# A Perceiver block on one Trainium2 core: ScalarE rounds the turned weights ahead of the next exponentials in the first half of each batch

## The chip, the cores and the metric

The kernel runs on one core of a Trainium2 chip. The metric is the device time of one execution in microseconds (us), the median over several runs.

## The reference

`x` is 64 sequences of 32 rows of 512 numbers, `ctx` is 64 sequences of 257 rows of 128. Three blocks follow each other, each on the layer-normed stream with a residual sum around it:

```python
x = x + xattn(layernorm(x), ctx, ...)   # 16 heads, latent queries and keys with rotary factors
x = x + attn(layernorm(x), ...)         # 16 heads of 32, weights from amp * cos(phase)
x = x + ffn(layernorm(x), ...)          # gates, two layers of folded products, layer norms
```

The change is in the middle of the first block. There, for a batch element b:

```python
scores  = einsum('hsr,hlr->hsl', q_r, k_r)     # 16 heads x 32 rows = 512 rows of 257 scores
weights = softmax(scores, axis=-1)
ctx_c   = einsum('hsl,ld->hsd', weights, kv_r)
```

and the result goes through an output product over all heads (`w_vo`).

## The kernel before

All operands of products are split into a high part (rounded to the float32r type) and a low part (value minus high), and a product is three matmuls (`multiply_parts`: high x high, high x low, low x high). ScalarE makes the high parts by a copy, VectorE or GpSimd the low parts by a subtraction (`low_part` on VectorE, line 77).

`query_path` carries the queries into DRAM. `cross_attention` then works through 64 batch elements, four to a tile of 128 output rows (`BT` = 4, `TILES` = 16). The 512 score rows of a batch element are taken in two halves of 256, each in two PSUM banks. So a tile has eight steps j = 0 to 7; step j belongs to batch `u = j // 2` and `half = j % 2`, and n counts steps over the whole stage. Below, a "first half" is an even step and a "second half" an odd one.

Each engine runs its own list of instructions in order, written out by hand, and waits on semaphores that count. In step n:

- **TensorE**: `score` of step n+1 (6 matmuls of 258 columns), `turn_weights` of step n (4 transposes of the normalised weights into the single bank `c_et_ps`; waits for `normed` of n and for `et_split` of n-1), in second halves `turn_kv` of the next batch, then `project` (matmuls of the output product of an earlier tile: one head in first halves, three heads in second halves), and in first halves `mix` of the batch before (6 matmuls).
- **ScalarE**: `exponential` of step n+1 (two activations with sums), `round_turned` of step n (reads `c_et_ps`), in second halves `round_kv`, `round_mixed` and `round_keys`, in first halves `round_queries`; at j = 4 also `square_row`.
- **VectorE**: `find_peak` of n+1, `keep_ends` of n, in first halves `split_kv`, in second halves `add_end` of the batch before, `normalise` of n+1 (a reciprocal and a product), `split_turned` of step n (the second reader of `c_et_ps`), at j = 2 `add_out` and at j = 6 `keep_moments`.
- **GpSimd**: rotates keys, takes the low parts of queries, keys and the mixed result.
- **SyncE**: all DMAs. The weight of key 257 goes through DRAM: after `keep_ends` of a second half, `store_ends` writes it, and `spread_ends` reads it back to all partitions; `add_end` of the next second half waits for it.

The last reader of `c_et_ps` gives the bank back:

```python
            def turn_weights(n, half):
                pe.wait_ge(normed, n + 1)
                wait(pe, et_split, n)
```

`c_sc_ps` has two banks for each half, and `c_et_ps` has one bank for both halves.

Of the kernel before, what the change touches and what calls it, by code (L numbers as in the profile page):

```python
# [42 lines left out]
def wait(engine, sem, value):  # L43

    if isinstance(value, int) and value <= 0:
        return
    engine.wait_ge(sem, value)
# [27 lines left out]
def low_part(nc, low, value, high):  # L75

    return nc.vector.tensor_tensor(low, value, high.bitcast(F32), ALU.subtract)  # L77
# [669 lines left out]
def cross_attention(nc, crossing, holo, x, q_dram, w_vo_dram, ends_dram, x1, spare, stat, ident, eps, half_pi, left_counted):  # L747
# [4 lines left out]
    with ExitStack() as ctx:  # L752
# [69 lines left out]
        def known(i, least):  # L822

            return not isinstance(i, int) or i >= least
# [94 lines left out]
        def _(dve):  # L919
            def find_peak(n, v):  # L920
                dve.wait_ge(scored, n + 1)
                wait(dve, exped, n - 1)
                nc.vector.tensor_reduce(peak[:, v], sc_ps[:, 2 * v:2 * v + 2, 0:L], AX_X, ALU.max, negate=True).then_inc(peaked, 1)  # L923
# [10 lines left out]
            def keep_ends(n, i, u, half):  # L934
                v = u % 2
                if half == 0:
                    wait(dve, ends_stored[v], 32 * i + 16 * (u // 2))
                nc.vector.tensor_tensor(ends[:, v, 2 * half:2 * half + 2], sc_ps[:, 2 * half:2 * half + 2, END], inverse[:, half],
                                        ALU.mult).then_inc(ended, 1)

            def split_turned(n, u, half):
                dve.wait_ge(et_rounded, n + 1)
                at = slice(2 * P * half, 2 * P * (half + 1))
                low_part(nc, e_t[1][:, u % 2, :, at], et_ps[:].rearrange("p (k x) -> p k x", k=2), e_t[0][:, u % 2, :, at]).then_inc(et_split, 1)

            def split_kv(b, u):
                dve.wait_ge(kv_rounded, b + 1)
                low_part(nc, kv[1][:, u], kv_ps[:, 0:2 * P].rearrange("p (k x) -> p k x", k=2), kv[0][:, u]).then_inc(kv_split, 1)

            def add_end(i, u):  # L950
                b, v = BT * i + u, u % 2
                dve.wait_ge(mix_done, b + 1)
                dve.wait_ge(ends_back[v], 32 * i + 16 * (u // 2) + 16)
                wait(dve, mix_split, b - 1)
                spread = ends_spread[:, v].rearrange("p (x c) -> p c x", c=CH)
                by_chunk = lambda a: a.rearrange("p (c x) -> p c x", c=CH)
                nc.vector.scalar_tensor_tensor(by_chunk(whole[:, v]), spread, kv_t[u][:, END:L], by_chunk(mix_ps[:]),
                                               ALU.mult, ALU.add).then_inc(mix_taken, 1)
# [15 lines left out]
            def tile(i, w):  # L974
                for j in range(STEPS):
                    n, u, half = STEPS * i + j, j // 2, j % 2
                    b = BT * i + u
                    more = not (isinstance(n, int) and n == PAIRS - 1)
                    if more:
                        find_peak(n + 1, 1 - half)  # L980
                    keep_ends(n, i, u, half)
                    if half == 0:
                        split_kv(b, u)
                    if half == 1 and (u or known(i, 1)):
                        add_end(i - (u == 0), (u - 1) % BT)
                    if more:
                        normalise(n + 1, 1 - half)
                    split_turned(n, u, half)
                    if j == 2 and known(i, 2):
                        add_out(i - 2)  # L990
                    if j == 6 and known(i, 2):
                        keep_moments(i - 2)
# [32 lines left out]
        @block.scalar  # L1025
        def _(act):
            def exponential(n, v):

                act.wait_ge(peaked, n + 1)
                for c in range(2):  # L1030
                    last = nc.scalar.activation(sc_ps[:, 2 * v + c, 0:L], sc_ps[:, 2 * v + c, 0:L], ACT.Exp, bias=peak[:, v, c:c + 1],  # L1031
                                                accum_out=total[:, v, c:c + 1])
                last.then_inc(exped, 1)

            def round_turned(n, b, u, half):
                act.wait_ge(turned, n + 1)
                if half == 0:
                    wait(act, mix_done, b - 1)
                nc.scalar.activation(e_t[0][:, u % 2, :, 2 * P * half:2 * P * (half + 1)], et_ps[:].rearrange("p (k x) -> p k x", k=2),
                                     ACT.Copy).then_inc(et_rounded, 1)  # L1040

            def round_kv(b, u):
                act.wait_ge(kv_turned, b + 1)
                wait(act, mix_done, b - BT + 1)
                nc.scalar.activation(kv[0][:, u], kv_ps[:, 0:2 * P].rearrange("p (k x) -> p k x", k=2), ACT.Copy).then_inc(kv_rounded, 1)

            def round_queries(b, u, t):
                act.wait_ge(q_loaded[u], queries_in(u, t))
                wait(act, scored, 2 * b - 2)
                nc.scalar.activation(q_high[:, u % 2], q[u].bitcast(F32), ACT.Copy).then_inc(q_rounded, 1)  # L1050

            def round_keys(b, u):
                act.wait_ge(rotated_, b + 1)
                wait(act, scored, 2 * b - 2)
                nc.scalar.activation(keys[0][:, u % 2], kv_even[u], ACT.Copy).then_inc(key_rounded, 1)

            def round_mixed(b, u, t, w):
                act.wait_ge(mix_taken, b + 1)
                if u == 0:
                    wait(act, out_done, t - 1)  # L1060
                nc.scalar.activation(mixed[0][:, w, :, u], whole[:, u % 2].rearrange("p (h s) -> p h s", h=H), ACT.Copy).then_inc(mix_rounded, 1)  # L1061

            def square_row(t):
                act.wait_ge(centred, t + 1)
                row = x1[:, bass.ds(t, 1)].rearrange("p t d -> p (t d)")
                if isinstance(t, int) and t == 0:
                    act.wait_ge(warmed, 1)
                nc.scalar.activation(scratch[:], row, ACT.Square, bias=neg_mean[:], accum_out=squares[:]).then_inc(squared, 1)

            def tile(i, w):  # L1070
                for j in range(STEPS):
                    n, u, half = STEPS * i + j, j // 2, j % 2
                    b = BT * i + u
                    if not (isinstance(n, int) and n == PAIRS - 1):
                        exponential(n + 1, 1 - half)
                    round_turned(n, b, u, half)
                    if half == 1 and not (isinstance(b, int) and b + 1 >= B):
                        round_kv(b + 1, (u + 1) % BT)
                    if half == 1 and (u or known(i, 1)):
                        round_mixed(b - 1, (u - 1) % BT, i if u else i - 1, w if u else 1 - w)  # L1080
                    if not (isinstance(b, int) and b + 2 >= B):
                        if half == 0:
                            round_queries(b + 2, (u + 2) % BT, i + (u + 2) // BT)
                        else:
                            round_keys(b + 2, (u + 2) % BT)
                    if j == 4 and known(i, 2):
                        square_row(i - 2)

            nc.scalar.activation(scratch[:, 0:1], ident[:, 0:1], ACT.Exp).then_inc(warmed, 1)
            round_keys(0, 0)  # L1090
            round_queries(0, 0, 0)
            exponential(0, 0)
            round_kv(0, 0)
            round_keys(1, 1)
            round_queries(1, 1, 0)
            in_tiles(act, tile)
            round_mixed(B - 1, BT - 1, TILES - 1, 1)
            act.wait_ge(holo_stepped, 12)
            nc.scalar.activation(holo.phase, holo.phase, ACT.Abs).then_inc(holo_cosined, 1)
            act.wait_ge(holo_cosined, 1)  # L1100
            nc.scalar.activation(holo.phase, holo.phase, ACT.Sin, bias=half_pi[:], scale=-1.0).then_inc(holo_cosined, 1)
            act.wait_ge(kept, TILES - 2)
            nc.scalar.activation(stat[:, 1, 0:TILES - 2], stat[:, 1, 0:TILES - 2], ACT.Sqrt, bias=eps[:], scale=1.0 / D).then_inc(rooted, 1)
            for t in (TILES - 2, TILES - 1):
                square_row(t)
# [1105 lines left out]
```

## Time and profile before

| | us |
|---|---|
| median of 3 runs | 1606.23 (1604.67 to 1607.58) |
| the profiled execution | 1605.91 |
| its span, first to last instruction | 1604.1 |
| full tiles of the attention loop, from j = 4 of tile 1 to j = 4 of tile 14 | 373.71 |
| the same, to the last transposes before the stop in tile 15 | 398.36 |
| one tile in the middle of it (801.00 to 829.70) | 28.70 |

In the span TensorE is busy 92%, VectorE 71%, ScalarE 54%, GpSimd 39%. Times inside the trace count from the start of the span. "T1" below stands for the four transposes of a first half, "T2" for those of a second half. A row of the timeline gives the start, the duration, the engine, the line, the operation with its output and inputs, how many instructions were merged, and in brackets the idle time of the engine in front of it with what ended it. Ends of matmuls are modelled.

### The profile page before, as it was taken

The page shows a single profiled execution, that of the slowest core. Times are in us where ns is not written, and L with a number is a line of the kernel's source. Part 1 is how long each engine was busy: PE and PEld are TensorE (multiplying, and loading weights), DVE is VectorE, ACT ScalarE, POOL GpSimd, SP SyncE. Part 2 cuts the span into 40 slices and gives each one's busy share as a digit, 9 for nine tenths or more (in the row PEclk, how much of TensorE's full clock was granted, in tenths as well). Part 3 has the DMA queues.
Part 4 walks back from the last instruction along what each step waited for, and adds up shares of the span by engine and source line. Part 5 has one row for each costly group of instructions (what it writes and reads, how often), then busy time and mean ns, then how long its engine had stood idle before and what let it go on. Part 6 is the DMA issues. An engine that isn't in the chain of part 4 may idle for free. (4 is left out here: it accounts for less than half of the span.)

```text
span 1604.1 us, 27410 instructions
## 1 busy us (share of the span) xinstructions
PE 1471.8 (92%) x8392; PEld 1134.6 (71%) x8392; DVE 1139.9 (71%) x1952; ACT 863.3 (54%) x1859; POOL 632.8 (39%) x596
## 2 busy tenths in 40 slices
PE   4799999999967999999999867999898899999997
PEld 3577777777746888888888656888443478787876
DVE  6888788887628888888888653777687735556466
ACT  4566566656546666666666533555211355554554
POOL 4244342542036777767677513221251202222021
PEclk9899999999979999999999978999898899999999
DMA  4223334243565555555555514000244100000000
GB/s 152 70 83 107 105 110 128 71 122 88 191 197 109 129 114 118 127 111 128 111 120 120 121 20 172 1 0 0 84 173 159 43 1 1 27 0 27 0 27 27
DMA packets 141207, 140.14 MB, mean 87 GB/s; under 512 B 84438, under 2 KB 112214, under 8 KB 139996
## 3 DMA queue, kind: packets, MB, share of 16 engines
q1 hardware_dynamic: 140572, 138.60, 31.9%
q10 hardware_dynamic: 576, 0.81, 0.2%
q8 instruction: 30, 0.49, 0.1%
q14 instruction: 29, 0.24, 0.1%
HBM read 109.88 MB, written 27.39 MB: 86 GB/s over the span
## 5 line engine op out<-in xcount | busy, mean ns | idle before, releaser
L1031 ACT ACTIVATE c_sc_ps<-c_sc_ps,c_peak 128x257 f32<-128x257 f32 x256 | 113.6, 444 | 156.9 <-DVE c_peak L923 156.9
L77 DVE TENSOR_TENSOR b_rot_parts_low<-b_rot,b_rot_parts_high 128x1536 fp32r<-128x1536 f32 x64 | 136.5, 2132 | 20.6 <-ACT b_rot_parts_high L543 20.6
L884 POOL TENSOR_TENSOR c_mixed_low<-c_whole,c_mixed_high 128x512 fp32r<-128x512 f32 x64 | 81.9, 1280 | 131.2 <-ACT c_mixed_high L1061 131.2
L280 POOL TENSOR_TENSOR b_turned_raw<-b_turn_part 128x384 f32<-128x384 f32 x32 | 69.0, 2155 | 163.5 <-DVE b_key_parts_low L77 162.2
L1627 PE MATMUL f_ps<-f_right,f_left 128*128 128x512 f32 x256 | 116.1, 615 | 8.3 <-ACT f_raw L1670 5.9
L70 PE MATMUL c_out_ps<-c_shared_high,c_mixed_high 128*128 128x512 f32 x256 | 112.6, 440 | 8.8 <-issue 8.8
L326 DVE TENSOR_TENSOR b_rot<-b_w_qr,b_angle 128x1536 f32<-128x1536 f32 x64 | 119.5, 1867 | 0.2
L923 DVE TENSOR_REDUCE c_peak<-c_sc_ps 128x2 f32<-128x514 f32 x128 | 88.5, 691 | 42.7 <-PE c_sc_ps L72 41.6
L70 PE MATMUL b_ps<-c_shared_high,b_wq_parts_high 128*128 128x512 f32 x256 | 108.6, 424 | 6.5 <-DVE c_shared_low L77 6.5
L276 POOL TENSOR_TENSOR b_turn_part<-b_early,b_centre 128x384 f32<-128x384 f32 x64 | 84.6, 1342 | 72.9 <-DMA b_early<-early 71.3
L70 PE MATMUL e_mm_ps<-folded_high,e_h_t_high 128*128 128x512 f32 x256 | 106.4, 416 | 6.7 <-DVE e_h_t_low L77 6.6
L1125 PE MATMUL c_et_ps<-ident,c_e 128*128 128x128 f32 x512 | 81.3, 282 | 32.9 <-DVE c_e_t_low L77 30.9
L543 ACT ACTIVATE b_rot_parts_high<-b_rot 128x1536 fp32r<-128x1536 f32 x64 | 95.3, 1489 | 24.5 <-PE b_ps L72 17.0
L1983 ACT ACTIVATE spare<-spare 128x512 f32<-128x512 f32 x64 | 46.3, 724 | 114.3 <-DVE spare L2050 114.3
L72 PE MATMUL b_ps<-c_shared_high,b_wq_parts_low 128*128 128x512 f32 x256 | 103.9, 406 | 0.0
L71 PE MATMUL b_ps<-c_shared_low,b_wq_parts_high 128*128 128x512 f32 x256 | 103.3, 404 | 0.0
L1627 PEld LDWEIGHTS f_ps<-f_right,f_left 128*128 128x128 f32 x256 | 50.0, 197 | 74.3 <-issue 65.1
L72 PE MATMUL c_out_ps<-c_shared_high,c_mixed_low 128*128 128x512 f32 x256 | 102.4, 400 | 0.0
L71 PE MATMUL e_mm_ps<-folded_low,e_h_t_high 128*128 128x512 f32 x256 | 102.3, 400 | 0.0
L72 PE MATMUL e_mm_ps<-folded_high,e_h_t_low 128*128 128x512 f32 x256 | 102.3, 399 | 0.0
L71 PE MATMUL c_out_ps<-c_shared_low,c_mixed_high 128*128 128x512 f32 x256 | 102.1, 399 | 0.0
L1863 POOL TENSOR_TENSOR spare<-spare,out_norm 128x512 f32<-128x512 f32 x15 | 20.8, 1389 | 200.5 <-DVE spare L2057 200.5
(244 smaller groups left out, 4291.1 us busy)
## 6 DMA issues: line engine op xcount, KB each, us to landing
c_ends_spread<-end_weights SPq DMA_DIRECT2D x64, 256.0 KB, 3.8
carried_queries<-x SPq DMA_DIRECT2D x7, 2048.0 KB, 11.2
b_early<-early SPq DMA_DIRECT2D x15, 640.0 KB, 4.0
c_raw<-cache_t SPq DMA_DIRECT2D x64, 128.5 KB, 3.4
c_swapped<-cache_t SPq DMA_DIRECT2D x128, 64.2 KB, 3.2
f_left<-ent_in SPq DMA_DIRECT2D x16, 512.0 KB, 5.5
f_right<-ent_out SPq DMA_DIRECT2D x16, 512.0 KB, 6.9
c_q_first<-carried_queries SPq DMA_DIRECT2D x32, 224.0 KB, 3.3
```

What stands on the lines that cost most here:

```text
L70: nc.tensor.matmul(out, left[0], right[0], start=start, stop=False)
L71: nc.tensor.matmul(out, left[0], right[1], start=False, stop=False)
L72: return nc.tensor.matmul(out, left[1], right[0], start=False, stop=stop)
L77: return nc.vector.tensor_tensor(low, value, high.bitcast(F32), ALU.subtract)
L276: nc.gpsimd.tensor_tensor(turn_part[:, n], key, centre[:, 2 * v + n].unsqueeze(2).to_broadcast(shape), ALU.mult).then_inc(key_multiplied, 1)
L326: nc.vector.tensor_tensor(rot[:, k % 2], weight, angles, ALU.mult).then_inc(rot_ready, 1)
L543: nc.scalar.activation(rot_parts[0][:, k % 2], rot[:, k % 2], ACT.Copy).then_inc(rot_rounded, 1)
L884: nc.gpsimd.tensor_tensor(mixed[1][:, w, :, u], whole[:, u % 2].rearrange("p (h s) -> p h s", h=H), mixed[0][:, w, :, u].bitcast(F32), ALU ...
L923: nc.vector.tensor_reduce(peak[:, v], sc_ps[:, 2 * v:2 * v + 2, 0:L], AX_X, ALU.max, negate=True).then_inc(peaked, 1)
L1031: last = nc.scalar.activation(sc_ps[:, 2 * v + c, 0:L], sc_ps[:, 2 * v + c, 0:L], ACT.Exp, bias=peak[:, v, c:c + 1], accum_out=total[:, v, ...
L1125: last = nc.tensor.transpose(et_ps[:, (2 * k + c) * P:(2 * k + c + 1) * P], e[:, half, c, k * P:(k + 1) * P], ident[:])
L1627: return nc.tensor.matmul(ps[:, m], left[:, slot, m * P:(m + 1) * P], right[:, slot], start=k == 0, stop=k == CF - 1)
```

## The change

In first halves ScalarE does `round_turned(n)` ahead of `exponential(n + 1)`, and VectorE does `split_turned(n)` right behind `keep_ends`, ahead of `split_kv` and `normalise(n + 1)`. Second halves keep their order. No instruction, semaphore, buffer or DMA is added or taken away.

```diff
@@ VectorE, tile(i, w), step j
                     keep_ends(n, i, u, half)
                     if half == 0:
+                        split_turned(n, u, half)
                         split_kv(b, u)
                     if half == 1 and (u or known(i, 1)):
                         add_end(i - (u == 0), (u - 1) % BT)
                     if more:
                         normalise(n + 1, 1 - half)
-                    split_turned(n, u, half)
+                    if half == 1:
+                        split_turned(n, u, half)
                     if j == 2 and known(i, 2):
                         add_out(i - 2)
@@ ScalarE, tile(i, w), step j
+                    if half == 0:
+                        round_turned(n, b, u, half)
                     if not (isinstance(n, int) and n == PAIRS - 1):
                         exponential(n + 1, 1 - half)
-                    round_turned(n, b, u, half)
+                    if half == 1:
+                        round_turned(n, b, u, half)
                     if half == 1 and not (isinstance(b, int) and b + 1 >= B):
                         round_kv(b + 1, (u + 1) % BT)
```

## Rows read from the trace of the kernel before

**Rows 1.** Windows, busy time by engine: 13 tiles, a batch of tile 0, four batches

```profile
core 0: us, PE busy (x) PEld busy (x) DVE busy (x) ACT busy (x) POOL busy (x), PEclk, DMA share, GB/s
513.40:887.11 373.71, 362.40 (x2081) 308.08 (x2081) 310.70 (x688) 249.92 (x752) 269.08 (x313) 1.00 0.56 120
485.60:491.96 6.36, 4.37 (x29) 3.71 (x29) 5.60 (x13) 4.63 (x14) 5.12 (x7) 1.00 0.66 134
801.00:807.92 6.92, 6.92 (x41) 5.93 (x41) 5.54 (x12) 5.34 (x16) 5.11 (x7) 1.00 0.51 106
807.92:814.89 6.97, 6.92 (x41) 5.94 (x41) 5.90 (x14) 4.64 (x14) 5.42 (x7) 1.00 0.64 121
814.89:822.00 7.11, 6.92 (x42) 5.92 (x41) 5.78 (x12) 4.64 (x14) 5.24 (x7) 1.00 0.71 149
822.00:829.70 7.70, 7.09 (x43) 5.91 (x41) 6.70 (x16) 4.63 (x14) 4.97 (x7) 1.00 0.42 96
```

**Rows 2.** Timeline of TensorE from 801 us, transposes alone: T1, T2, T1, T2

```profile
801.00 0.63 PE L1125 MATMUL c_et_ps<-ident,c_e 128*128 128x128 f32 x4 [0.42 <-DVE c_e_t_low L77]
...
804.30 0.60 PE L1125 MATMUL c_et_ps<-ident,c_e 128*128 128x128 f32 x4
...
807.92 0.63 PE L1125 MATMUL c_et_ps<-ident,c_e 128*128 128x128 f32 x4
...
811.40 0.63 PE L1125 MATMUL c_et_ps<-ident,c_e 128*128 128x128 f32 x4
```

**Rows 3.** Timeline of VectorE: a second half, a first half, and around add_out

```profile
804.50 0.69 DVE L923 TENSOR_REDUCE c_peak<-c_sc_ps 128x2 f32<-128x514 f32 x1 [0.47 <-PE c_sc_ps L72]
...
805.18 1.13 DVE L957 SCALAR_TENSOR_TENSOR c_whole<-c_ends_spread,c_kv_t,c_mix_ps 128x512 f32<-128x512 f32 x1
...
808.65 0.41 DVE L77 TENSOR_TENSOR c_kv_low<-c_kv_ps,c_kv_high 128x256 fp32r<-128x256 f32 x1
809.76 0.17 DVE L928 RECIPROCAL c_inverse<-c_total 128x2 f32<-128x2 f32 x1 [0.69 <-ACT c_sc_ps L1031]
809.96 0.69 DVE L931 TENSOR_TENSOR c_e<-c_sc_ps,c_inverse 128x512 f32<-128x512 f32 x1
810.57 0.68 DVE L77 TENSOR_TENSOR c_e_t_low<-c_et_ps,c_e_t_high 128x512 fp32r<-128x512 f32 x1
...
825.39 0.68 DVE L965 SCALAR_TENSOR_TENSOR x<-c_out_ps,x 128x512 f32 x1
...
826.28 0.69 DVE L923 TENSOR_REDUCE c_peak<-c_sc_ps 128x2 f32<-128x514 f32 x1
```

**Rows 4.** Timeline of ScalarE: an exponential of a second half, then a first half

```profile
805.23 0.45 ACT L1031 ACTIVATE c_sc_ps<-c_sc_ps,c_peak 128x257 f32<-128x257 f32 x1 [1.01 <-DVE c_peak L923]
...
808.70 0.45 ACT L1031 ACTIVATE c_sc_ps<-c_sc_ps,c_peak 128x257 f32<-128x257 f32 x1 [0.86 <-DVE c_peak L923]
...
809.62 0.60 ACT L1039 ACTIVATE c_e_t_high<-c_et_ps 128x512 fp32r<-128x512 f32 x1
810.10 0.64 ACT L1050 ACTIVATE c_q_high<-c_q_first 128x512 fp32r<-128x512 f32 x1
```

**Rows 5.** Timeline, last transposes of the stage: TensorE, then rounding, then low part

```profile
937.40 0.63 PE L1125 MATMUL c_et_ps<-ident,c_e 128*128 128x128 f32 x4 [0.72 <-DVE c_e_t_low L77]
...
938.06 0.60 ACT L1039 ACTIVATE c_e_t_high<-c_et_ps 128x512 fp32r<-128x512 f32 x1 [1.84 <-PE c_et_ps L1125]
...
938.69 0.69 DVE L77 TENSOR_TENSOR c_e_t_low<-c_et_ps,c_e_t_high 128x512 fp32r<-128x512 f32 x1 [0.20 <-ACT c_e_t_high L1039]
```

**Rows 6.** SyncE's queue from 805 us: the end weights out and back

```profile
805.44 0.36 SPq L831 DMA_DIRECT2D end_weights<-c_ends  x1
...
807.85 0.45 SPq L837 DMA_DIRECT2D c_ends_spread<-end_weights  x1
```

**Rows 7.** Tile c_ends_spread, 515 to 911 us: idle time before its reader (us, times)

```profile
  issue: 2.5, 5
  DMA c_ends_spread<-end_weights: 0.9, 3
...
DMA to landing us min/median/max: 3.3/3.8/5.1
```

## The prediction

> **What bounds the kernel now.** I read the busy times by window first. From 513.40 to 887.11, in 13 tiles, TensorE is busy 362.40 of 373.71 us at the full granted clock, so it is near its limit, and 3% is left [rows 1]. A clean tile is 28.70 us: four batches of 6.92, 6.97, 7.11 and 7.70. TensorE's busy time is 6.92 in the first three and 7.09 in the last, while the work is the same; the extra length lies in waits. In tile 0, where there is no output product yet, TensorE is busy 4.37 of 6.36 us: there a chain through the other engines sets the pace.
>
> Next I read where TensorE waits: at the transposes, for the low part of the transposes before [rows 2]. The order of one step on VectorE tells why. A step begins with `find_peak` and ends with `split_turned`, and the next transposes start 3.42 us after the peak began, in second halves (804.50 to 807.92) [rows 2, 3]. In first halves it is the same 3.42 from 807.98, where the peak began 0.06 after T1, to T2 at 811.40. But the contents differ. A second half has no gap: `add_end` of 1.13 us fills the time of the exponentials. A first half has a gap of 0.69 us, in which VectorE waits for the exponentials (809.76), and the low part of T1, ready to be made long before, comes last (810.57 to 811.25) [rows 3]. T2 starts 0.15 after it.
>
> TensorE alone needs less: after a T1 that had to wait itself, T2 comes 3.30 later with no wait (801.00 to 804.30) [rows 2]. After T2 its work lasts 3.49 (811.40 to the batch end at 814.89 [rows 1]). So TensorE's floor is 6.79 a batch.
>
> **The change part by part.** Let T1 start at 0.
>
> *New first half.* The rounding can start when the transposes are done. The last step of the stage is the one where ScalarE stands ready for them: rounding at 0.66, low part at 0.66 + 0.63 = 1.29 [rows 5]. `keep_ends` is over by then (its peak begins at 0.06 to 0.20 and both take about 0.8). On ScalarE the exponentials start 0.48 after the rounding (809.62 to 810.10), at 1.14; that is later than now, where they start when the peak is found, at 0.78 (808.70 less 807.92) [rows 2, 4]. From the first exponential to the reciprocal it takes 1.06 (808.70 to 809.76), so ScalarE lets VectorE go on at 2.20 [rows 3, 4]. On VectorE the low part takes 0.61 until the next one begins (as 809.96 to 810.57 shows for a product of that size), `split_kv` begins at 1.90 and ends at 2.31. The next one may begin 0.07 ahead of that end, at 2.24. So the reciprocal begins at 2.24, bounds 2.20 and 2.31. Product 0.20 later, at 2.44; it ends at 3.13, and T2 can start 0.15 behind it, at 3.28 (3.24 to 3.35).
>
> TensorE arrives at 3.30. So the wait for the low part goes, its successor is the wait for `normed`, and it ends within 0.1 of TensorE's own arrival. The exponentials of the second half are 0.36 later than before, and nothing pays for it up to there.
>
> *What is late next.* `score` of the next step stands ahead of T2 in TensorE's order, and ends 0.16 after T2's natural start; the next peak begins 0.20 after that start (804.30 to 804.50), at 3.50 [rows 2, 3]. VectorE is free for it at 2.44 + 0.61 = 3.05. The second half keeps its order and its 3.42. So T1 to T1 is 3.50 + 3.42 = 6.92, above TensorE's 6.79. That is what the first batch of the tile already does (6.92) [rows 1]; the change brings the next two to it, which gains 0.05 and 0.19.
>
> *The batch with `add_out`.* It holds VectorE for 0.89 (825.39 to 826.28) and the peak behind it is what makes this batch 7.70 [rows 1, 3]. It would now start at 3.05 instead of 3.39 (825.39 less 822.00). Peak at 3.94, next T1 at 7.36: a gain of 0.34. The two small copies of `keep_moments` have the 0.45 from 3.05 to 3.50 to themselves.
>
> *Sum.* A clean tile becomes 3 x 6.92 + 7.36 = 28.12, a gain of 0.58. From 513.40 to 911.76, where the last tile stops for its DMAs, are 398.4 us, 13.9 tiles of 373.71 / 13 = 28.75: 8.1 us. The bounds of T2 move only the last batch of a tile, by up to 0.07: 1.0 us.
>
> *Taken off.* In tile 0, T1 to T1 is now 6.36. New, VectorE is free for the peak at 3.05, and 3.42 later is 6.47: 0.11 lost in each of about 6 batches, 0.6 us. Then the end weights. `add_end` waits for them in 8 of 55 batches already, 3.4 us in all [rows 7]. In a clean batch they are stored at 805.44, read back at 807.85 and, with the median landing of 3.8, there at 811.65; `add_end` comes at 812.06, some 0.4 later [rows 6, 7]. Batches of 7.0 to 7.1 shrink to 6.92, and landings go up to 5.1. Where the DMA rules, a batch gives back what it gained. I take 12 of 55 (bounds 8 and 25), that is 1.8 us (1.2 to 3.7).
>
> Moving the rounding costs ScalarE and its other work nothing: `round_queries` starts 0.3 later (2.20 against 1.90), and ScalarE waits some 1 us for the next peak anyway (1.01 ahead of 805.23) [rows 4]. SyncE and GpSimd are moved past nothing.
>
> 8.1 - 0.6 - 1.8 = 5.7 us. The profiled execution took 1605.91, its span 1604.1; it lies 0.3 below the median of the runs. Forecast **1600.2**.
>
> **A rule weighed.** VectorE instructions start about 0.07 before the recorded end of the one before (809.96 + 0.69 is 810.65, the next starts at 810.57) [rows 3]. The Trainium skill, VectorE: DVE Perf Modes, section "The DRAIN you can't avoid", says that the next operation does not start until the pipe is empty. By that the two hand-overs of the new order would add 0.14, T2 could start at 3.42, and the gain would be 5.7 less 14 x 0.14, 3.7 us: an estimate by the page, which the trace's overlap speaks against.
>
> **The rivals.** *The end weights take it all.* If the average batch waits 0.15 more for its DMA, 55 x 0.15 = 8.2 us is lost, and the time is 1605.9 + 0.6, about **1606**. For it: the slack is 0.4 and the landings spread by 1.8; waits exist [rows 7]. Against it: the first batch of each clean tile has run at 6.92 and does not wait. With a loss of 5 us or more the change can't be told from none.
>
> *T2 is late: slower.* The exponentials now stand behind T1, the rounding and its latency, one chain from T1 to T2: 3.28 by my sum. TensorE needs 3.49 after T2, so the chain costs nothing until 6.92 - 3.49 = 3.43. Past that each 0.1 costs all 55 batches 5.5 us, and the gain is gone at about 3.43 + 0.58 / 4 = 3.58. It takes one hand-over or one slowed exponential 0.3 above its row. At 3.80 a batch is 7.29, the one with `add_out` 7.88, the tile 29.75, and the time 1606 + 13.9 x 1.05, about **1620**. Against it: each link has its row, the one that never waits in the middle of the stage, transposes to rounding, included [rows 5]. The new order lets VectorE read `c_et_ps` while ScalarE works in `c_sc_ps`; today `add_end` reads `c_mix_ps` beside the exponential of 805.23, which takes the same 0.45 as the one of 808.70 beside the shorter `split_kv` [rows 3, 4]. For it: it is the longest chain that the change makes, from five links that were never seen in this order.
>
> **How the numbers follow.** Forecast 0.60, end weights 0.25, late T2 0.15. A difference under 0.2% (3.2 us) can't be told from no change with this kernel. The forecast's own range is 8.1 + 0.5 - 0.6 - 1.2 = 6.8 at best to 8.1 - 1.0 - 0.6 - 3.7 = 2.8: 1599 to 1603. The range reaches to the end weights' case and somewhat below the best sum, since runs of one kernel spread by 1.5 to each side: 1597 to 1607. That leaves out the late T2. Faster 0.60, same 0.25, slower 0.15.
>
> **What the changed profile would show.** Right: T1 to T2 3.3 us throughout; the transposes wait for the low part only in first halves; batches of 6.92, 6.92, 6.92 and 7.36; the reciprocal of a first half has no long wait; the rounding 0.66 after T1. Wrong: T2 waiting for the product `c_e` with more than 3.43 after T1, or exponentials over 0.45 us (late T2); `add_end` waiting for `c_ends_spread` in most batches (end weights); a TensorE that takes longer than 3.30 and 3.49 with no waits.

## The result and the profile after

The changed kernel takes 1598.86 us (median of 6 runs, 1596.45 to 1600.63) against 1606.45 for the kernel before (1604.67 to 1607.76): a ratio of 0.9951 with a 95% interval of 0.9939 to 0.9964, that is 5.8 to 9.8 us less. Forecast was 1600.2, in a range of 1597 to 1607. The profiled execution took 1599.37, its span is 1597.5.

Busy time by windows in the changed kernel: 12 full tiles, one clean tile, and its four batches, the last with `add_out`.

```profile
542.72:881.41 338.69, 331.74 (x1921) 284.13 (x1921) 286.98 (x637) 231.15 (x696) 249.52 (x289) 1.00 0.59 122
712.27:740.31 28.04, 27.60 (x160) 23.65 (x161) 23.92 (x54) 19.27 (x58) 20.75 (x25) 1.00 0.59 122
712.27:719.17 6.90, 6.90 (x40) 5.92 (x41) 5.54 (x12) 5.34 (x16) 5.10 (x7) 1.00 0.59 121
719.17:726.06 6.89, 6.89 (x42) 5.90 (x41) 5.91 (x14) 4.64 (x14) 5.32 (x7) 1.00 0.48 107
726.06:732.97 6.91, 6.91 (x42) 5.93 (x41) 5.79 (x12) 4.65 (x14) 5.11 (x7) 1.00 0.72 161
732.97:740.31 7.34, 6.90 (x41) 5.91 (x41) 6.69 (x16) 4.64 (x14) 5.22 (x7) 1.00 0.55 100
```

Against [rows 1] the batches of 6.92, 6.97, 7.11 and 7.70 are now 6.90, 6.89, 6.91 and 7.34. TensorE's busy time fills three of them; in the last it still has a gap. But busy time counts the modelled ends of matmuls and hides short waits. In the changed kernel T2 starts 0.12 behind the start of the last score product (715.43 to 715.55), where nothing holds it; T1 starts 0.25 behind it:

```profile
718.92 0.28 PE L72 MATMUL c_sc_ps<-c_key_high,c_q 128*128 128x258 f32 x1
719.17 0.63 PE L1130 MATMUL c_et_ps<-ident,c_e 128*128 128x128 f32 x4
```

The low part of the T2 before it runs on VectorE from 718.34 to 719.02, and T1 follows 0.15 later. So the second half is still paced by VectorE: its peak at 715.75 plus 3.42 is 719.17.

The same 12 tiles of the kernel before, which the comparisons below use:

```profile
542.11:887.11 345.00, 334.55 (x1921) 284.38 (x1921) 286.90 (x637) 231.36 (x696) 248.84 (x289) 1.00 0.56 119
```

One first half in the timeline of the changed kernel, transposes at 712.27:

```profile
712.27 0.63 PE L1130 MATMUL c_et_ps<-ident,c_e 128*128 128x128 f32 x4 [0.41 <-DVE c_e_t_low L77]
...
712.93 0.60 ACT L1041 ACTIVATE c_e_t_high<-c_et_ps 128x512 fp32r<-128x512 f32 x1 [0.75 <-PE c_et_ps L1130]
...
713.42 0.45 ACT L1033 ACTIVATE c_sc_ps<-c_sc_ps,c_peak 128x257 f32<-128x257 f32 x1
...
713.56 0.69 DVE L77 TENSOR_TENSOR c_e_t_low<-c_et_ps,c_e_t_high 128x512 fp32r<-128x512 f32 x1 [0.77 <-ACT c_e_t_high L1041]
...
714.17 0.42 DVE L77 TENSOR_TENSOR c_kv_low<-c_kv_ps,c_kv_high 128x256 fp32r<-128x256 f32 x1
...
714.50 0.16 DVE L928 RECIPROCAL c_inverse<-c_total 128x2 f32<-128x2 f32 x1
...
714.69 0.69 DVE L931 TENSOR_TENSOR c_e<-c_sc_ps,c_inverse 128x512 f32<-128x512 f32 x1
...
715.55 0.60 PE L1130 MATMUL c_et_ps<-ident,c_e 128*128 128x128 f32 x4
...
715.75 0.69 DVE L923 TENSOR_REDUCE c_peak<-c_sc_ps 128x2 f32<-128x514 f32 x1 [0.37 <-PE c_sc_ps L72]
```

Counted from T1, the rounding starts at 0.66, the exponentials at 1.15, the low part at 1.29, `split_kv` at 1.90, the reciprocal at 2.23, the product at 2.42, T2 at 3.28 and the next peak at 3.48. The prediction had 0.66, 1.14, 1.29, 1.90, 2.24, 2.44, 3.28 and 3.50. The gap of 0.69 ahead of the reciprocal [rows 3] is gone, and a gap of 0.77 stands ahead of the low part, where VectorE waits for the rounding; T2 waits for nothing. TensorE's waits for VectorE in the loop are now those of T1.

**Where the time went, by place.** All from the two traces, first transposes of the stage to the last ones: 466.63 us before (470.77 to 937.40), 459.24 after (473.56 to 932.80), 7.4 less. Of it 6.2 lie in the 13.9 tiles (398.36 before, 514.67 to 906.84 after), 1.5 in the opening of the stage (42.63 against 41.11), 0.4 in the stop of the last tile, and 0.7 are lost behind it. The stages ahead of it took 2.8 more in this execution and those behind it 2.0 less, with no edit in either. So the 6.2 of the tiles is what this pair of traces shows of the new order in the loop; the stages around it differ by 2 to 3 us between executions though their code is the same.

### The profile page after: what moved, and what is told of

It is laid out like the page before. It is cut to its first block and busy times, and to the rows that moved or that the text cites. A ratio compares the mean times of both kernels' runs of the same rounds, so it can differ in the third digit from the quotient of the medians.

```text
span 1597.5 us, 27410 instructions
## 1 busy us (share of the span) xinstructions
PE 1467.7 (92%) x8392; PEld 1134.8 (71%) x8392; DVE 1138.1 (71%) x1952; ACT 863.4 (54%) x1859; POOL 633.5 (40%) x596
## 5 line engine op out<-in xcount | busy, mean ns | idle before, releaser
L77 DVE TENSOR_TENSOR c_e_t_low<-c_et_ps,c_e_t_high 128x512 fp32r<-128x512 f32 x128 | 87.9, 686 | 41.0 <-ACT c_e_t_high L1041 40.9
L1041 ACT ACTIVATE c_e_t_high<-c_et_ps 128x512 fp32r<-128x512 f32 x128 | 76.4, 597 | 56.6 <-PE c_et_ps L1130 56.6
```

## The experiments

**1. Each half of the change alone.** Two kernels: ScalarE's new order with VectorE's old one, and the reverse. Both are shown against the changed kernel.

```diff
@@ e1: ScalarE as in the change; VectorE stays
-                    if half == 0:
-                        split_turned(n, u, half)
-                        split_kv(b, u)
+                    if half == 0:
+                        split_kv(b, u)
...
-                    if half == 1:
-                        split_turned(n, u, half)
+                    split_turned(n, u, half)
@@ e2: VectorE as in the change; ScalarE stays
-                    if half == 0:
-                        round_turned(n, b, u, half)
...
-                    if half == 1:
-                        round_turned(n, b, u, half)
+                    round_turned(n, b, u, half)
```

> The change on ScalarE alone: rounding ahead of the exponentials in first halves, VectorE in its old order (low part of the turned weights last). My theory: both halves of the change are needed; the exponentials come later and the low part still stands behind the product. T1 to T2 is then 2.20 + 0.20 + 0.61 + 0.68 + 0.15 = 3.84, T1 to T1 7.33, the batch with add_out 7.93, a tile 29.9 against 28.70 before: about 1606 + 17, and 4 more in tile 0, so 1623 to 1627. Rival: the early rounding carries the gain, VectorE's order is secondary: 1599 to 1603.

> The change on VectorE alone: the low part of the turned weights ahead of the key's low part and the product in first halves, with ScalarE rounding behind the exponentials as before. My theory: VectorE waits for the rounding at 2.5 after T1, all the rest follows, T2 at 4.5, T1 to T1 8.0, with add_out 8.6, a tile 32.6: about 1606 + 54 + 8 = 1668. Rival: TensorE waits mainly for the low part, and getting it off the end of the half is what pays: below 1606.

Measured in one run each, beside 1604.33 for the kernel before: ScalarE alone **1623.94**, VectorE alone **1647.90**. A first half of the first kernel and the start of the next second half:

```profile
701.48 0.60 PE L1128 MATMUL c_et_ps<-ident,c_e 128*128 128x128 f32 x4
...
703.65 0.17 DVE L928 RECIPROCAL c_inverse<-c_total 128x2 f32<-128x2 f32 x1 [0.89 <-ACT c_sc_ps L1031]
703.85 0.69 DVE L931 TENSOR_TENSOR c_e<-c_sc_ps,c_inverse 128x512 f32<-128x512 f32 x1
704.46 0.68 DVE L77 TENSOR_TENSOR c_e_t_low<-c_et_ps,c_e_t_high 128x512 fp32r<-128x512 f32 x1
...
705.29 0.63 PE L1128 MATMUL c_et_ps<-ident,c_e 128*128 128x128 f32 x4 [0.41 <-DVE c_e_t_low L77]
```

T1 to T2 is 3.81 here (3.81 to 3.90 in other batches) and 3.84 in tile 0, expected 3.84; the high part lay ready from 702.71 while VectorE idled 0.89. So the early rounding has no worth by itself. Its price is the later exponentials, and VectorE must spend the time on the low part.

In the second kernel VectorE waits for a rounding that comes late:

```profile
706.20 0.63 PE L1127 MATMUL c_et_ps<-ident,c_e 128*128 128x128 f32 x4 [0.47 <-DVE c_e_t_low L77]
...
708.23 0.69 DVE L77 TENSOR_TENSOR c_e_t_low<-c_et_ps,c_e_t_high 128x512 fp32r<-128x512 f32 x1 [1.51 <-ACT c_e_t_high L1041]
...
710.11 0.65 PE L1127 MATMUL c_et_ps<-ident,c_e 128*128 128x128 f32 x4 [0.47 <-DVE c_e L931]
```

The direction was as expected, but the expected time was 20 us too high. T1 to T2 is 3.91 here, and not 4.5: T1 waited for VectorE, whose next peak (705.97) began ahead of it, so that the exponentials started at 0.49 and not at 0.78. In the three other batches of a tile T1 was not held up, and T1 to T2 is 4.35. Both rivals fall: neither half carries the gain.

**2. The trip of the end weights.** Both orders without the store to DRAM and the load back. `add_end` still runs and adds zeros, so these kernels leave out what key 257 contributes.

```diff
@@ e3 (order before) and e4 (order after), SyncE and VectorE
-                        store_ends(i - 1, u)
...
-                        spread_ends(i - 1, u)
...
-                dve.wait_ge(ends_back[v], 32 * i + 16 * (u // 2) + 16)
...
@@ GpSimd, once ahead of the loop
+            nc.gpsimd.memset(ends_spread[:], 0.0).then_inc(spread_set, 1)
```

> The kernel before without the trip of the end weights through DRAM: no store, no load back, VectorE adds a constant zero row in their place (so key 257 does not contribute to the mixed values). My theory: the trip costs little here; 12 tiles from T1 of tile 2 to T1 of tile 14 take 344.4 (12 x 28.70) against 345.0 with it. The stop of 10 us in the last tile, where add_end waits behind the loads of the next stage, goes in great part. Rival: the waits of the loop come from the other DMAs, and stay without the trip.

> The changed kernel without the trip of the end weights through DRAM, as above (key 257 does not contribute). My theory: the waits for the trip took back 2 us of what the new order gains; the 12 tiles take 336.6 (12 x 28.05) against 338.7 with it, so the distance between the two orders is 7.8 here and 6.3 with the trip. Rival: the irregular tiles come from other DMAs or from GpSimd; 338 to 339 stays.

Measured in one run each: **1591.45** in the old order, **1582.94** in the new one, 8.5 apart. The 12 tiles by windows, first the old order, then the new one:

```profile
541.55:885.85 344.30, 334.10 (x1920) 284.34 (x1921) 286.87 (x637) 231.10 (x696) 248.86 (x289) 1.00 0.31 83
```

```profile
539.88:876.38 336.50, 331.51 (x1921) 284.23 (x1921) 286.99 (x637) 231.45 (x696) 249.52 (x289) 1.00 0.32 85
```

Expected were 344.4 and 336.6. The irregular tiles are gone with the trip. It costs 0.7 us of the 12 tiles in the old order (345.00) and 2.2 in the new one (338.69), so 1.5 of the gain of 7.8 went to it. That most of the total, 13 to 16 us, comes off in both lies outside the 12 tiles: a long wait ahead of `add_end` in the last tile is there with the trip in both orders (9.9 and 9.5 us), and the step is 4.3 us long in place of 13.9 and 13.5 without it.

The waits in the changed kernel, tile `c_ends_spread`, 515 to 911 us (idle time of its reader, times):

```profile
  issue: 2.4, 4
  DMA c_ends_spread<-end_weights: 0.4, 2
...
DMA to landing us min/median/max: 3.2/3.9/4.8
```

Six waits of 2.8 us in all against eight of 3.4 in [rows 7]: there are not more of them, but each costs more. In the 12 tiles of the old order they sum to 3.1 us and the trip costs 0.7; in the new order they sum to 1.5 (1.9 with three of 0.10 to 0.15) and it costs 2.2. The likely reason, not tried by a run of its own, is that a batch of 6.90 has next to no other wait that they could fall together with. In the two kernels of experiment 1, with batches of 7.3 and more, there is a single such wait over the same stretch, of 0.2.

**3. How much room the new chain has.** An idle copy on ScalarE between the rounding and the exponentials of each first half.

```diff
@@ e5 (128 columns), e6 (448 columns), ScalarE
                     if half == 0:
                         round_turned(n, b, u, half)
+                        for _ in range(1):
+                            nc.scalar.activation(idle[:, 0:448], idle[:, 448:448 + 448], ACT.Copy)
```

> The changed kernel with one idle copy of 128 columns on ScalarE between the rounding and the exponentials of each first half (about 0.19 us more on the chain from T1 to T2). My theory: tile 0 of the changed kernel shows the bare chain, 3.17 from T1 to T2, and TensorE and VectorE leave it room up to 3.43; 3.36 still fits. Batches stay at 6.90, only the one with add_out grows by 0.19: 12 tiles take 2.3 more, 341.0; the whole about 3 more than the changed kernel, 1602. Rival: no slack, each batch pays 0.19: 12 tiles take 9 more, 347.8, and the time is above the kernel before.

> The same with an idle copy of 448 columns, about 0.47 us more. My theory: T1 to T2 is 3.17 + 0.47 = 3.64, 0.21 over the limit of 3.43: batches of 7.13 and 7.81 with add_out, a tile 29.2; 12 tiles take 350.4, and the whole is about 1616. So the first 0.26 are free, and what is over counts fully. Rival: each batch pays the whole 0.47: a tile 29.9, 12 tiles 359.

Each of the delayed kernels was run once. Measured: the long one **1613.90** where about 1616 was expected, its 12 tiles 352.40 (expected 350.4) and a clean tile of 29.25 (expected 29.2). Its chain ends in a wait of T2 for the product:

```profile
705.78 0.60 PE L1136 MATMUL c_et_ps<-ident,c_e 128*128 128x128 f32 x4
...
706.99 0.57 ACT L1082 ACTIVATE c_idle<-c_idle 128x448 f32<-128x448 f32 x1
...
708.70 0.69 DVE L934 TENSOR_TENSOR c_e<-c_sc_ps,c_inverse 128x512 f32<-128x512 f32 x1
...
709.45 0.66 PE L1136 MATMUL c_et_ps<-ident,c_e 128*128 128x128 f32 x4 [0.25 <-DVE c_e L934]
```

The short one took **1603.80**, 5 more than the changed kernel where 3 were expected, and its 12 tiles 344.66 where 341.0 were. The steps fit: 715.60 to 718.96 is 3.36, 718.96 to 722.50 is 3.54, together 6.90 as without the delay.

```profile
715.60 0.63 PE L1136 MATMUL c_et_ps<-ident,c_e 128*128 128x128 f32 x4 [0.47 <-DVE c_e_t_low L77]
718.96 0.66 PE L1136 MATMUL c_et_ps<-ident,c_e 128*128 128x128 f32 x4
722.50 0.63 PE L1136 MATMUL c_et_ps<-ident,c_e 128*128 128x128 f32 x4
```

Whether the rest was the end weights or a slack that is not there was asked of one more kernel, the short delay without the trip:

> The changed kernel with the short idle copy of 128 columns on ScalarE (about 0.19 us on the chain from T1 to T2) and without the trip of the end weights through DRAM (key 257 does not contribute). With the trip the 12 tiles took 344.7, and 341.0 had been expected; clean tiles in that trace are 28.29. My theory: the 5 us over 12 x 28.29 = 339.5 are waits for the end weights and go with the trip: 339 to 340 here, that is 3 over the 336.5 of the changed kernel without the trip. Rival: the slack is not there and part of the delay is paid in every batch: 343 or more.

Measured: **1590.11**, and the 12 tiles by window:

```profile
544.30:883.04 338.74, 333.14 (x1920) 284.54 (x1921) 291.36 (x637) 240.53 (x744) 249.27 (x289) 1.00 0.31 84
```

338.74 against 336.50 is 2.2 for a delay of 0.19 in 48 first halves, which would be 9 if each one paid. The slack is there: of the four batches of a tile two stay at 6.90 and 6.89, the one ahead of `add_out` takes 6.95 and the one with it 7.49 for 7.34. The other 5.9 us of the short delay's trace (344.66 less 338.74) go with the trip of the end weights; 5.2 of them show there as waits ahead of `add_end`.

**4. VectorE's order and the mean of `add_out`.** First `split_kv` goes back ahead of `split_turned`; then, on top of it, the small product that makes the negative mean moves from the end of j = 2 to behind `keep_ends` of j = 4 (for the last two tiles it stays where it was).

```diff
@@ e7 and e8, VectorE
-                        split_turned(n, u, half)
                         split_kv(b, u)
+                        split_turned(n, u, half)
@@ e8 only: add_out ends behind its first instruction
                     keep_ends(n, i, u, half)
+                    if j == 4 and known(i, 2):
+                        find_mean(i - 2)
...
```

> The changed kernel with split_kv back ahead of split_turned in first halves: it fits into the 0.4 us in which VectorE waits for the rounding (from 0.9 to 1.3 after T1). My theory: the reciprocal then waits for ScalarE alone and starts at 2.20 in place of 2.23, and the chain T1 to T2 has slack anyway: same as the changed kernel within 0.5 us, 1598 to 1599. Rival: VectorE's load is the limit of first halves, and filling its gap shortens every batch: 1594 or less.

> The same, and the small product of add_out that makes the negative mean moved from the end of j = 2 into the gap of VectorE at j = 4. My theory: VectorE's 0.89 of add_out stand on the path of the last batch of each tile, and this takes 0.2 of it away: that batch 7.14 in place of 7.34, 13 tiles x 0.2 = 2.6 us, the time 1596. Rival: the batch with add_out is held by TensorE or by the wait for the output product, and nothing changes.

Measured: `split_kv` first **1598.81** (ratio to the kernel before 0.9958, interval 0.9945 to 0.9972), no different from the changed kernel. With the mean moved **1595.35** (0.9929, interval 0.9915 to 0.9942). Both once more, in one session with the changed kernel:

> The changed kernel once more, beside the next one. My theory: 1598.9 within 1 us, ratio 0.995; a second trace has the same clean tile of 28.05 from T1 to T1, and its irregular tiles lie elsewhere. Rival: the irregular tiles are fixed in place by the program.

> The kernel with split_kv first and the mean of add_out moved into the gap of j = 4, once more. My theory: 2.5 to 3.5 us below the changed kernel measured beside it. Rival: the distance seen before (1598.8 against 1595.4) was chance, and the two agree within 1 us.

Measured: the changed kernel **1597.97** (0.9949, interval 0.9936 to 0.9963), with the mean moved **1593.83** (0.9918, interval 0.9905 to 0.9932). It beats both kernels: by 3.5 us the one with `split_kv` first, measured beside it, and by 4.1 us the changed one, measured beside it in the second session, where no run of either reaches into the range of the other (at most 1594.60 against at least 1596.46). The end of j = 2 in it, VectorE's timeline:

```profile
733.00 0.69 DVE L931 TENSOR_TENSOR c_e<-c_sc_ps,c_inverse 128x512 f32<-128x512 f32 x1
733.61 0.68 DVE L965 SCALAR_TENSOR_TENSOR x<-c_out_ps,x 128x512 f32 x1
734.21 0.08 DVE L965 DVE_READ_ACCUMULATOR x<-c_out_ps,x 128x1 f32 x1
734.21 0.69 DVE L923 TENSOR_REDUCE c_peak<-c_sc_ps 128x2 f32<-128x514 f32 x1
...
738.21 0.14 DVE L971 TENSOR_SCALAR c_neg_mean<-c_row_sum 128x1 f32<-128x1 f32 x1
```

`add_out` now holds the peak up by 0.60 and not 0.89 [rows 3], as the read of the sum runs beside the peak; the T2 to T1 step behind it is 3.76 where it was 4.07, and 13 tiles x 0.3 are 3.9 us. Expected had been 0.2 a tile.

In the second trace of the changed kernel the clean tile is again 28.03, and the 12 tiles take 339.44. Two of the waits for the end weights are at the same places (603.7 and 617.8 in the first trace, 603.6 and 617.7 in the second), others are not. These two belong to the 18th and the 20th `add_end` of the stage, and the same two wait in all eight traces that have the trip, the kernel before included (604.5 and 618.8), but for the two of experiment 1 with their longer batches. So part of the waits is bound to the program, against the theory; what sets them was not tried.

## Why the prediction was right

**What bounds the kernel.** Right, and it is shown. T2 waited for the low part of T1 because it stood last in VectorE's list. With it moved the step from T1 to T2 is TensorE's own, 3.26 to 3.30 in all 48 first halves of the 12 tiles. That the batch then stays at VectorE's 3.48 + 3.42 = 6.90, above TensorE's floor of 6.79, holds too (718.92 and 719.17 above).

**Both edits as one.** The prediction costed them together; experiment 1 shows that each alone costs 20 and 44 us.

**The chain and the next bound.** The chain has its links within 0.02 of the sum up to the product. The prediction put its end at 3.28 and TensorE's arrival at 3.30, "within 0.1" of each other. Tile 0, where TensorE is early, shows the bare chain: 3.17.

```profile
493.83 0.63 PE L1130 MATMUL c_et_ps<-ident,c_e 128*128 128x128 f32 x4 [1.55 <-DVE c_e_t_low L77]
...
497.00 0.66 PE L1130 MATMUL c_et_ps<-ident,c_e 128*128 128x128 f32 x4 [0.42 <-DVE c_e L931]
```

The 0.15 behind the product was too much: that was the row of a wait for the low part. Behind the product it is 0.06 (496.25 + 0.69 to 497.00). The limit was off the other way. The prediction set it at 3.43, 6.92 less the 3.49 that TensorE needs behind T2. When T2 comes late by the product, TensorE needs about 3.54, with nothing in front of T1 (718.96 to 722.50 with the short delay, 709.45 to 713.00 with the long one), and 6.90 less 3.54 is 3.36. So the rival "T2 is late" had 0.19 of room (3.17 to 3.36), where the prediction had 0.15 and the expectations of experiment 3 had 0.26. The short delay just fits. With +0.47 the three batches without `add_out` take 7.22, 7.16 and 7.11, a mean growth of 0.26 and not of 0.47, where 0.21 had been expected.

**The sizes.** A clean tile gained 0.66 (28.70 to 28.04), the prediction had 0.58: 0.02 less in each of the four batches (6.90 for 6.92, 7.34 for 7.36). That is 1.1 us over 13.9 tiles. The end weights were taken at 1.8 us for 13.9 tiles, 1.55 for 12; the 12 tiles show 1.5 in this pair of traces, and 2.2 with the second trace of the changed kernel (339.44). Together the 13.9 tiles gained 6.2, where 6.3 were forecast. That this agrees to 0.1 is luck in part, for two terms were off in opposite directions. At the clean tile's 0.66 the 13.9 tiles would have gained 9.2 and not 8.1; 3.0 of it were lost and not 1.8. Half of that loss lies behind the 12 tiles: the last 0.9 tile (887.11 to 911.76 before, 881.41 to 906.84 after) became 0.8 longer, with one long wait ahead of `add_end` in it.

```profile
893.98 1.13 DVE L957 SCALAR_TENSOR_TENSOR c_whole<-c_ends_spread,c_kv_t,c_mix_ps 128x512 f32<-128x512 f32 x1 [1.29 <-issue]
```

The prediction also expected more waits (12 for 8); there were 6, each of them dearer. One reading in it was wrong without bearing on the sum: `round_queries` started 2.18 after T1 in the kernel before (810.10 less 807.92), not 1.90, and starts at 2.05 now, which is earlier and not 0.3 later.

**Tile 0.** The loss of 0.11 a batch was 0.08 (3.27 + 3.17 = 6.44 against 6.36). But the opening of the stage as a whole did not lose 0.6, it gained 1.5 in this pair of traces, and that is the main part of the difference between the 5.7 forecast and the 7.4 of the stage. The four steps at its start by window, before and after:

```profile
470.77:485.60 14.83, 11.72 (x50) 9.87 (x51) 10.45 (x24) 8.87 (x28) 9.06 (x12) 0.64 0.50 95
```

```profile
473.56:487.39 13.83, 10.71 (x50) 8.94 (x51) 10.26 (x24) 8.87 (x28) 9.05 (x12) 0.70 0.50 102
```

TensorE does the same 50 matmuls in both at a mean granted clock of 0.64 and 0.70 of full speed. The clock had fallen to its lower level (0.50, that is 1.2 of 2.4 GHz) ahead of the stage in both traces, at 461.1 and 461.4 us; TensorE had been busy 1.39 of the 6.00 us ahead of that in the one and 3.34 of 6.30 in the other, and then for 0.00 us up to 466. It came back to 1.00 at 481.6 and 481.8 us, at nearly the same moment of the execution, while the stage began 2.8 us later in the second trace. So 10.8 us of the stage fell into the low clock before and 8.3 after. The step from 477.55 to 481.98 of the kernel before shows the price: TensorE is busy for all of its 4.43 us at a mean clock of 0.55. That the stage began later is not the edit's doing, for nothing is changed up to the first transposes. So this part of the gain is most likely luck of the pair, and so is that only the kernel before fell to the lower level once more (505.5 to 508.9). Whether the new order adds anything stays open, for no run separates the two: over the four other traces of the new order with the trip and without a delay the opening varies from 40.0 to 42.2 us, and in the old order without the trip it is 41.8, in the midst of them.

**The end weights as the rival that takes it all.** Wrong in size, right as a mechanism: it took 1.5 to 2.2 us of the 12 tiles in these traces, 3.0 of the 13.9 tiles, and 5.9 of the 12 tiles in the one with the short delay.

**The rule on the VectorE pipe.** By the Trainium skill, VectorE: DVE Perf Modes, section "The DRAIN you can't avoid", as the prediction read it, the gain was estimated at 3.7 us. The same section adds that "A next op that is not held starts earlier", and that is what the trace shows for these instructions: 713.56 + 0.69 is 714.25 and `split_kv` starts at 714.17, 714.17 + 0.42 is 714.59 and the reciprocal starts at 714.50. The batch with `add_out`, which by the rule would be 0.14 longer than summed, is 7.34 where 7.36 were summed.

## What to carry to other kernels

When two engines each have a job for the other inside one step, moving one of them alone can make the chain longer, as it did here in both cases; lay out both orders from one common event and look which engine idles at which moment, then fill that gap with what the consumer waits for. Work out the bare length of the new chain and the limit up to which it costs nothing, since that margin tells more than the gain does. And look for small tails ahead of the critical instruction: here a product of 0.15 us and its wait, moved past the peak, gave 3.5 to 4.1 us, half as much again as the 7.6 of the change itself.

## What was not expected of the hardware

TensorE's transposes started 0.15 us after the end of the low part (705.37 + 0.68 to 706.20 in the second kernel of experiment 1), but 0.06 after the end of the product (709.36 + 0.69 to 710.11 in the same trace). The accumulator's read of `add_out` (0.08) does not hold up the next reduction, which starts at the same 734.21. And two waits for one DMA trip recur at the same two of its 64 uses in eight traces of six programs, while its landing times between 515 and 911 us of the traces range from 3.2 to 5.5 us.
